# Splitting two experts' weights in the conv, a third staging place, and a new order of jobs in the attention turns

## What is computed

```python
x = x + conv(_gn(x))     # 1x1 conv over 192 channels and 28 correlations of a pixel with its neighbours
t = tokens(x)            # 8 x 256 tokens of 192
t = t + attn(_ln_t(t))   # causal, one head, no output projection
t = t + ffn(_ln_t(t))    # top-1 of 8 experts: (silu(t W1) * (t W2)) W3, F = 469
```

## Time and profile before

| | us |
|---|---|
| median of 3 runs (233.23 to 236.65) | 234.15 |
| the profiled execution | 233.54 |
| its span on the core | 231.7 |
| conv, to the first `take_xt` of the turns | 0 to 60 |
| attention turns and gating | 60 to 127 |
| expert slots | 127 to 221 |

### The profile page before, as it was taken

The page is one execution under the profiler, slowest core; times in us unless marked ns, Lnnn a source line. Parts: engine busy times, 40 slices in busy tenths (PEclk is TensorE's granted clock), DMA queues, the critical chain, the costliest instruction groups (busy, mean ns, idle before and its releaser), DMA issues.

```text
span 231.7 us, 4547 instructions
## 1 busy us (share of the span) xinstructions
PE 209.1 (90%) x1331; PEld 182.4 (79%) x1331; DVE 171.4 (74%) x559; ACT 113.9 (49%) x244; POOL 105.3 (45%) x133
## 2 busy tenths in 40 slices
PE   6999799989899969998888799999999999999950
PEld 3686588968799958887665688898999999999940
DVE  3577897768399769699877789997767686868640
ACT  2276585175499697996640134343343333343410
POOL 4245756545439996896665103223131313131221
PEclk9999999999999999999999999999999999999995
DMA  6992247665730663647212332332001000000000
GB/s 218 366 350 87 83 126 187 170 219 165 252 135 0 237 234 117 221 188 259 81 52 63 80 86 70 93 83 78 21 14 37 17 34 20 34 17 22 33 20 0
DMA packets 16343, 26.46 MB, mean 114 GB/s; under 512 B 3795, under 2 KB 12673, under 8 KB 15424
## 3 DMA queue, kind: packets, MB, share of 16 engines
q1 hardware_dynamic: 14448, 22.65, 30.7%
q0 software_dynamic: 1872, 3.52, 4.4%
HBM read 19.76 MB, written 6.76 MB: 114 GB/s over the span
## 4 chain that ended last, share of the span: by engine, by line
PE 59%; DVE 16%; POOL 6%; issue 6%; DMA 6%; ACT 5%; POOLq 1%; DVEq 0%; ACTq 0%
PE bank L1468 8%; PE bank L1146 4%; PE bank L1333 4%; PE bank L1150 4%; PE bank L1149 4%; PE bank L1148 4%; PE bank L1147 4%; PE bank L1429 4%; PE bank L1469 3%; DMA stage<-in_w_all 2%; PE bank L1446 2%; PE bank L1192 2%; DMA taps_sb<-near_rows 2%; DMA out_rows<-yo,rows 1%; PE bank L1141 1%
## 5 line engine op out<-in xcount | busy, mean ns | idle before, releaser
L498 POOL DMA_INDIRECT out_rows<-yo,rows x23 | 23.2, 1011 | 76.9 <-DVE yo L1107 61.5
L1468 PE MATMUL bank<-wall,HH 128*128 (+1 forms) x88 | 28.1, 374 | 0.3 <-issue 0.3
L667 ACT ACTIVATE HH<-bank 128x512 fp32r<-128x512 f32 x23 | 13.8, 599 | 27.8 <-PE bank L1429 27.7
L1089 DVE TENSOR_TENSOR gh<-gh,bank 128x470 f32<-128x470 f32 x23 | 14.8, 645 | 14.5 <-PE bank L1150 14.4
L673 ACT ACTIVATE FH<-bank 128x256 fp32r<-128x256 f32 x23 | 8.9, 385 | 27.5 <-PE bank L1446 27.5
L1469 PE MATMUL bank<-wall,HL 128*128 (+1 forms) x88 | 22.1, 251 | 0.0
L1146 PE MATMUL bank<-wall,FH 128*128 (+1 forms) x46 | 19.3, 419 | 1.6 <-DVE FL L1092 1.6
L464 POOL DMA_INDIRECT token_rows<-rows,posi x16 | 16.9, 1055 | 7.3 <-issue 4.0
L670 ACT ACTIVATE gh<-bank 128x470 f32<-128x470 f32 x23 | 13.0, 565 | 13.1 <-PE bank L1150 13.1
L1278 PE MATMUL bank<-mH 128*128 128x512 f32 x73 | 19.3, 400 | 0.0
L1084 DVE TENSOR_TENSOR HL<-bank,HH 128x512 fp32r<-128x512 f32 x23 | 15.9, 691 | 3.6 <-ACT HH L667 3.4
(11 more groups left out here) (247 smaller groups left out, 647.4 us busy)
## 6 DMA issues: line engine op xcount, KB each, us to landing
stage<-in_w_all SPq DMA_DIRECT2D x7, 1324.0 KB, 5.7
rows<-token_rows SPq DMA_DIRECT2D x23, 98.0 KB, 2.0
near_rows<-gram SPq DMA_DIRECT2D x8, 243.0 KB, 3.2
xcm<-in_x_cm SPq DMA_DIRECT2D x2, 768.0 KB, 8.3
rows<-in_x_tm SPq DMA_DIRECT2D x1, 1536.0 KB, 14.0
stage<-in_w_all SPq DMA_DIRECT2D x4, 331.0 KB, 4.0
token_rows<-emptyt SPq DMA_DIRECT2D x3, 294.0 KB, 4.2
taps_sb<-near_rows SPq DMA_DIRECT2D x8, 103.0 KB, 2.1
```

The source lines that it names most:

```text
L498: pool.indirect_dma_start(out=out, out_offset=bass.IndirectOffsetOnAxis(ap=rows[:, j, C + 2:C + 3].bitcast(U32), axis=0), in_=yo[:, par], ...
L1468: nc.tensor.matmul(dst[:, 0:2 * C], HH[:, 1 - par, k], w(0, P, c0, c0 + 2 * C), start=(k == 0), stop=False)
```

## The change

- A third staging place; expert e is staged in place e % 3, and its load waits for the split of expert e - 3.
- Expert 0 is loaded at the start, behind the inputs, in four parts; expert 1 in passes 2 to 5; expert 2 behind the last taps, and expert 3 as soon as expert 0 is split.
- Expert 0 is split in passes 5 to 8 of the conv (ACT, POOL, DVE) and expert 1 in its last passes. Expert 2's part 0 is copied by ACT in the last pass, ahead of turn 1, its rest in turn 1. Expert 3 is split in turns 1 and 2, expert 4 in turns 2 and 3, expert 5 in turns 4 and 5 (`SPLITS`). Experts 6 and 7 get their high copies in turns 8 and 9.
- ACT's turn: `norm_image(t)` stands ahead of the exponentials, `take_v` ahead of the copy to `PT`; `weights_hi(2, e)` goes behind that copy.
- PE's turn: `values` stands right behind `project`, ahead of the transposes of the probabilities; `turn_image(t)` ahead of the products with `V`; `fill(5)` becomes `fill(3)`.
- DVE's turn: `low_xt` ahead of the reciprocal. The pieces of `low_weights` are spread over slots -1 to 5.
- Start: POOL's memset of `taps` first, PE waits for it alone and runs `keep_busy(4)`. Slot 0: `fill(8)` becomes `fill(5)`.

```diff
-SPLIT_LAST = EXPERTS - 2
+STAGES = 3
+SPLITS = {0: 2, 1: 3, 2: 4, 4: 5}
...
+            for part in range(FIRST_PARTS):
+                weights_part(0, part)
             sp.wait_ge(empty_ready, 1)
             for b in range(IMAGES):
                 gram_to(b)
                 if 2 <= b < 2 + FIRST_PARTS:
...
+                    weights_part(1, b - 2)
...
                 taps_from(b)
-            weights_in(1)
-
-            for e in range(2, EXPERTS):
-                sp.wait_ge(wall_lo, e - 1)
-                sp.wait_ge(wall_q, e - 1)
+            weights_in(2)
+
+            for e in range(STAGES, EXPERTS):
+                sp.wait_ge(wall_lo, e - STAGES + 1)
+                sp.wait_ge(wall_q, e - STAGES + 1)
                 weights_in(e)
...
+                if b == IMAGES - 3:
+                    weights_lo(0, ((0, FE),))
                 if b == IMAGES - 2:
+                    weights_lo(0, ((FE, W12),))
                     token_factors(0)
+            weights_lo3(0)
             token_factors(1)
-            pool.wait_ge(wall_q, 1)
-            weights_lo(0)
+            pool.wait_ge(wall_q, 2)
+            weights_lo(1)
+            weights_lo3(1)
+            weights_lo(2)
             token_factors(2)
+            weights_lo3(2)
...
-                if t < SPLIT_LAST:
-                    weights_lo(t)
+                if t in SPLITS:
+                    weights_lo(SPLITS[t])
+                    weights_lo3(SPLITS[t])
...
             def step(t, par):
+                e = SPLITS.get(t - 1)
                 if on(t, 0):
                     take_xt(t, par)
-                if 1 <= t - 1 < EXPERTS - 1:
-                    weights_hi(1, t - 1)
-                    weights_hi(2, t - 1)
+                if e is not None:
+                    weights_hi(1, e)
+                if on(t, -1):
+                    if t == 2:
+                        sc.wait_ge(ln1_ready, 3)
+                    norm_image(t)
                 if on(t, 1):
...
                 if on(t, 0):
                     take_u(t, par)
+                    take_v(t, par)
                 if on(t, 1):
                     sc.wait_ge(pt_ready, t + AHEAD)
                     nc.scalar.activation(PT[:], bank[4][:, 0:3 * P], ACT.Copy).then_inc(pt_copied, 1)
-                if on(t, -1):
-                    if t == 2:
-                        sc.wait_ge(ln1_ready, 3)
-                    norm_image(t)
-                if on(t, 0):
-                    take_v(t, par)
-                if 1 <= t < EXPERTS:
-                    weights_hi(0, t)
-                if t == IMAGES:
-                    weights_hi(1, EXPERTS - 1)
-                    weights_hi(2, EXPERTS - 1)
+                if e is not None:
+                    weights_hi(2, e)
+                if t in SPLITS:
+                    weights_hi(0, SPLITS[t])
+                if t >= IMAGES:
+                    for part in range(3):
+                        weights_hi(part, t - 2)
...
+                if 5 <= i < IMAGES:
+                    weights_hi(i - 5, 0)
...
                 if i == IMAGES:
-                    weights_hi(1, 0)
+                    weights_hi(1, 1)
                 if i == IMAGES + 1:
-                    weights_hi(0, 0)
-                    weights_hi(2, 0)
+                    weights_hi(0, 1)
+                    weights_hi(2, 1)
+                if i == IMAGES + 3:
+                    weights_hi(0, 2)
...
-                if 2 <= t <= SPLIT_LAST:
-                    leftover(t - 1)
+                if t - 1 in SPLITS:
+                    leftover(SPLITS[t - 1])
...
                 if 2 <= t < IMAGES:
-                    fill(5)
+                    fill(3)
                 if on(t, 0):
                     project(t, par)
+                    values(t, par)
...
                     mm.then_inc(pt_ready, 1)
-                if on(t, 0):
-                    values(t, par)
+                if on(t, -1):
+                    turn_image(t)
...
                 if j == 0:
-                    fill(8)
+                    fill(5)
```

More of the change, by code:

```diff
@@ L242, in build @@
         cm_in = [sem(f"cm_in{g}") for g in range(len(GANGS))]
-        stage_in = [sem("stage_in0"), sem("stage_in1")]
+        stage_in = [sem(f"stage_in{n}") for n in range(STAGES)]
         empty_out = sem("empty_out")
@@ L370, in _ @@
         def _(pool):
+            nc.gpsimd.memset(taps[:].rearrange("p b h c -> p (b h c)"), 1.0).then_inc(filled, 1)
             nc.gpsimd.memset(half_c[:], -0.5).then_inc(filled, 1)
@@ L836, in leftover @@
                 w = wall[CB:P, e, 2 * W12:3 * W12]
-                nc.vector.tensor_tensor(w, stage[CB:P, e % 2, W12:2 * W12], w.bitcast(F32), ALU.subtract).then_inc(wall_q, 1)
+                nc.vector.tensor_tensor(w, stage(e)[CB:P, W12:2 * W12], w.bitcast(F32), ALU.subtract).then_inc(wall_q, 1)
             def gate(g, link):
@@ L895, in link @@
                     ve.wait_ge(dve2, LINKS * t + done[0])
+                if on(t, 0):
+                    low_xt(t, par)
                 if on(t, 2):
@@ L900, in step @@
                     link(nc.vector.reciprocal(rsum[:], ssum[:]))
-                if on(t, 0):
-                    low_xt(t, par)
                 if on(t, 1):
@@ L999, in _ @@
                     token_stats(1)
+                    leftover(0)
                 if i == IMAGES + 1:
@@ L1006, in _ @@
                     ve.wait_ge(ln1_ready, 2)
-                    leftover(0)
+                    leftover(1)
                 if i == IMAGES + 3:
@@ L1333, in keep_busy @@
                     nc.tensor.matmul(bank[6][:, 0:3 * P], some[:, 0:P], some[:, 0:3 * P], start=True, stop=True)
-            pe.wait_ge(filled, 4)
-            keep_busy(3, taps[:].rearrange("p b h c -> p (b h c)"))
+            pe.wait_ge(filled, 1)
+            keep_busy(4, taps[:].rearrange("p b h c -> p (b h c)"))
             pe.wait_ge(group_in, 16)
```

72 lines of the change are left out of this document (43 added, 29 removed).

## The result

The changed kernel is slower, by about 2%; I had forecast +0.6% as the likeliest and 231.5 to 238.5 us as the range. Put on the 234.15 us that the forecast was measured from, 1.0196 is 238.7 us, just above that range; the median of 238.2 and the profiled execution's 237.07 lie inside it.

The account below looks back on a forecast made before the run. ScalarE and TensorE were taken as full in the attention turns. Turns, with the later start and norm wait, end +2.9; slots give -0.5 and -0.4: +2.0 on 233.54, so 235.5 us (+0.6% on the median), range 231.5 to 238.5.

Parts of the forecast that it names:

- The 1.0 of delay from POOL is hidden under this wait.: Conv's end: POOL's half split of expert 0 delays the last images about 1.0, covered by the wait for expert 2's load.
- The load's chain: Attention start: expert 2's load issued 55.5, landing 61.2, copy 0.9, so `take_xt(1)` starts at 62.1 instead of 60.06: +2.0.
- Factors start 70.7, ready 73.8.: Turn 1: POOL begins the norm factors of images 3 to 7 at 70.7, needs 3.1, and has them at 73.8.
- The wait costs 2.5.: ACT's norm waits for the factors ahead of the exponentials, which start at 74.7 instead of 72.2.
- `leftover(2)` delays the factors by 1.15.: Turn 1: VectorE's new `leftover(2)` adds 1.15 before POOL can begin the norm factors.
- Rival 4: Chance 0.08: TensorE's 1.9 us idle at the norm wait drops the clock to 1.2 GHz, costing one turn's 5.95; 241.
- A plain turn of 6.75, PE waiting 0.8 for `PT`.: From one `project` start (p) to the next: 6.75 us, PE's output products waiting 0.8 for the turned probabilities' copy.
- p4 to p5: forecast 7.2: Turn 4: counts behind PE's outputs, then positions and `low_xt`, put the project starts at p4 = 87.4 and p5 = 94.6.
- Turn 6: POOL late by 0.6.: POOL's expert 5 rest, scatters and token root end at 104.7; `gate(1)` needs them, VectorE there about 0.6 earlier; p7 = 109.1.
- Slots -0.9.: Expert slots: -0.5 from `fill(5)` in place of `fill(8)`, some -0.4 from spreading the pieces over more slots.
- Where I would be wrong: The forecast fails if the project of image 7 starts before 107 or after 111.
- Rivals 1 to 3: Norm wait hidden (0.2): 233.0; turns take PE's own length (0.1): 232.3; two loads share the queue (0.07): 241.2.

Follow-up runs that it names:

- conv_tail: Changed kernel with `leftover(0)` behind the second norm factors and POOL's second piece of expert 0 behind the conv's last spread; 1.0000 of the kernel before.
- rests_late: Changed kernel with VectorE's rests of experts 2, 3, 4 and 5 moved from turns 1, 2, 3, 5 to 2, 3, 5, 5; 1.0064 of before.
- weights_only: Changed kernel with the turn order of before put back on ScalarE, TensorE and VectorE; 1.0139 of the kernel before.
- scatter_first: Changed kernel with GpSimd's rests of expert 5 put behind turn 4's scatters and token root; 1.0078 of the kernel before.
- after_again: The changed kernel unaltered, measured once more beside the kernel before; 1.0168 of it.
- combined: Changed kernel with conv_tail's and scatter_first's edits, `leftover(2)` behind token statistics, turn 2's norm put back, expert 2's first two copies behind the probabilities' copy; 0.9918 of before.
- order_only: Kernel before with only the change's turn order and `fill(3)`; weights, stages and slots as before; 0.9994 of the kernel before.

## Why the prediction was wrong, step by step

- **"The 1.0 of delay from POOL is hidden under this wait."** This is the step that failed. The structure was a maximum of two chains, and I priced one from rows and the other at half an instruction. The load's chain was right (+1.86 measured in conv_tail, +2.0 forecast). POOL's chain was 2.57, not 1.0: the piece's 1.21, 0.94 for the 2-column operation beside `leftover(0)`, and 0.42, the rest, with the low clock. Behind it comes the copy `weights_hi(0, 2)` all the same, 0.9, which I had counted behind the load alone; so even at my 1.0 the two chains were nearly level, and nothing was left to hide in. I wrote that the copies and `leftover(0)` "fall into waits"; DVE's did, but it held POOL's operation ahead of the last spread, which I never looked at. `take_xt(1)` came at 63.12 in place of 62.1, 3.6 later than before against the third taps copy.
- **Factors start 70.7, ready 73.8.** Measured 72.17 and 75.3: `low_u` of turn 1 began at 67.26 in place of 65.9, 1.0 of it from `take_xt(1)` and the rest with the clock low from 65. The increments of the sum held: 1.15 for `leftover(2)` against 1.14, and 3.1 for POOL.
- **The wait costs 2.5.** ACT's wait is 2.54 and 3.35 in the two executions, but putting the norm back gives only 1.3. With the norm behind the probabilities' copy the turn is 7.7, longer than the 6.7 of the earlier trace rows that I had compared it with. In that trace PE waits 0.96 for the probabilities' copy and 0.28 for the low part; no run separates the 1.0 further.
- **`leftover(2)` delays the factors by 1.15.** Right, and incomplete: it stands ahead of `low_xt(2)` too, so that p1 to p2 was 0.9 longer for it alone (rests_late).
- **Rival 4, the clock, 0.08.** This is the second step that failed: the sum has no term for the clock beside the waits. It happened in part, together with the main case and not in its place. I had argued against it from ACT's 1.80 of waiting at 81.21, behind which the clock had held. That row was true and no proof: the same program keeps or loses its clock at one and the same idle. The price was 1.5 in turn 2 and 0.6 in turn 1, not one turn's 5.95, since the clock came back after some 4 us. The Trainium skill (TensorE: Matmul & The Clock Gate, "HAM oscillation") warns of waits between bursts of matmuls, longer ones in its example than the 1.78 us here. The clock fell here behind these shorter ones, and 1.00 from 44 to 90 in the profiled execution of weights_only, with nearly as much idle in 44 to 51 (4.83 busy of 7), shows that it need not follow.
- **A plain turn of 6.75, PE waiting 0.8 for `PT`.** p3 to p4 is 6.70, p5 to p6 6.80. The wait is 0.52, and the rest lies in PE's own steps. p4 to p5: forecast 7.2, measured 7.32.
- **Turn 6: POOL late by 0.6.** The gate waited 0.76, and scatter_first gave back 0.46, or 0.99 against after_again, where DVE waits 0.5 longer for the counts; why is open.
- **Slots -0.9.** Measured -1.12 and -1.10.
- **Where I would be wrong:** if the project of image 7 starts "after 111". It started at 112.14 (106.57 before), and of the 3.0 us against the forecast 109.1, 2.9 were there at project 3 (83.53 against 80.65). Of these 2.9, 1.0 came at `take_xt(1)` and 1.2 were there at `take_xt(3)` (80.34 against 79.1); the other 1.6 lie between `take_xt(3)` and project 3, where the outputs and scores ran at the lower clock. Of the signs that I named, one failed: `weights_hi(0, 2)` did not wait for its load.
- **The total came out better than its terms.** At `xf` of slot 22 the changed kernel stood 2.9 later than the sum has it (218.20 against 215.3), and its profiled execution ended only 1.6 above the forecast 235.5. The difference is luck: the last stores took 1.3 less than in before's profiled execution.
- **Rivals 1 to 3.** The wait was not hidden, the turns did not take PE's own length, and the two loads back to back did not slow each other: `weights_hi(0, 2)` never waited in the changed kernel, and in conv_tail, where it did, expert 2 was there 5.8 after its issue (54.23 to 60.01), as one load alone.

## What to carry to other kernels

When two delays are said to be hidden under each other, work both out to the same depth: the cheap one, priced loosely, was the one that bound. Work put into an engine's idle time is free only if no other engine runs a critical step beside it; here 1.14 us of VectorE in a wait cost GpSimd 0.94 on the critical chain. And place such pieces by looking at both engines' lists: the same rest took 1.13 in turn 1 of the changed kernel and 2.23 in combined, beside GpSimd's. What taking it away gives depends on the next bound: 0.9 in the first (rests_late), 0.24 in the second (8.90 to 8.66), where ScalarE's four copies came next.

## What the runs showed of the hardware

**VectorE's subtraction of two SBUF tiles and GpSimd's instructions exclude each other.** DVE's subtraction of two SBUF tiles (64x940) took 1.14 us alone, 2.23 behind one of POOL's, and 3.00 in order_only, whose timeline shows the two alternate (DVE and POOL):

```profile
87.55 2.21 POOL L434 TENSOR_TENSOR wall<-stage,wall 128x940 fp32r<-128x940 f32 x1 [1.32 <-ACT wall L549]
87.75 3.00 DVE L836 TENSOR_TENSOR wall<-stage,wall 64x940 fp32r<-64x940 f32 x1
89.71 2.71 POOL L437 TENSOR_TENSOR wall<-stage,wall 128x768 fp32r<-128x768 f32 x1
92.72 0.39 PE L1233 MATMUL bank<-XH,mH 128*128 128x256 f32 x1 [2.49 <-DVE XH L799]
```

POOL's first ends at 89.76; DVE's ends 1.0 later, at 90.75; POOL's second, 1.83 alone, ends 1.67 after that. In these rows the first to start took no longer than alone. It goes both ways: a 128x16 subtraction of DVE took 1.06 in place of 0.17 in the changed kernel, at 44.84, behind POOL's piece of 44.65. An addition of DVE with one input from PSUM kept its time beside POOL's subtraction (0.56 at 57.26 in the kernel before, 0.55 elsewhere). The Trainium skill (SBUF — State Buffer, "SBUF: two separate sides") calls the pair of ports that the two share an exclusive lock and not a bandwidth split, for a VectorE instruction with two SBUF inputs against a GpSimd one that reads SBUF; these rows agree, down to an operation of 2 columns that waits 0.94 us.

**The granted clock is not a function of the program.** after and after_again are one program: 0.66 in 64 to 69 and in 78 to 83 of the one, 1.00 in the same stretches of the other. The windows of after_again:

```profile
64.00:69.00 5.00, 3.82 (x30) 3.56 (x31) 3.32 (x9) 4.59 (x13) 1.49 (x1) 1.00 0.74 256
69.00:75.00 6.00, 5.13 (x38) 4.50 (x36) 5.46 (x25) 2.51 (x4) 3.01 (x6) 1.00 0.02 7
75.00:78.00 3.00, 1.01 (x8) 0.72 (x7) 0.79 (x3) 2.97 (x11) 3.00 (x2) 1.00 0.25 39
78.00:83.00 5.00, 4.50 (x32) 4.17 (x33) 3.92 (x11) 4.77 (x11) 4.45 (x5) 1.00 0.75 275
```

PE is as idle in 75 to 78 as in the execution that lost its clock there (1.01 busy against 1.22), and its single waits are alike (1.92 and 1.33 against 1.78 and 1.48). What decides between the two stays open. It follows that one profile of a kernel with such idles is off by up to 2 us in the turns either way, and that the steps of the table above are compared only where their clocks are alike.
